# Masking with a byte written into a bf16: TensorE's constant pass left out, key weights scaled by a power of two

## The reference

```python
U = min(L, int(FACTOR * math.log(L)))                # 5 * ln 512 -> 31
Q, K, V = proj(Wq, bq), proj(Wk, bk), proj(Wv, bv)   # 16 x 16 heads x 512 x 16
scores = jnp.einsum('bhqd,bhkd->bhqk', Q, K) / math.sqrt(D)
top_vals, _ = jax.lax.top_k(scores, U)
thresh = top_vals[..., -1:]
scores = jnp.where(scores < thresh, -jnp.inf, scores)
attn = jax.nn.softmax(scores, axis=-1)
x = _layernorm(x + context @ Wo.T + bo)
gate, up = x @ wg.T, x @ wu.T                        # weights are int32 / 127
x = _layernorm(x + (silu(gate) * up) @ wd.T)
```

## Time and profile before

| | |
|---|---|
| median of 3 runs | 3387.09 us (3374.43 to 3392.51) |
| the profiled execution's own time | 3384.81 us |
| its span | 3383.0 us |
| granted TensorE clock, mean | 0.913 |
| busy: PE, DVE, ACT, POOL | 83%, 76%, 71%, 71% |
| tiles per run | 1024, so 3.30 us of span for each |

### The profile page before, as it was taken

One profiled execution on the slowest core, in us unless ns is written; L12 is line 12 of the kernel. 1 busy time (PEld: TensorE's weight loads), 2 busy tenths in 40 slices (PEclk: granted clock), 3 DMA queues, 4 the chain that ended last, 5 costly groups with the idle time before them and its releaser, 6 DMA issues.

```text
span 3383.0 us, 82396 instructions
## 1 busy us (share of the span) xinstructions
PE 2808.2 (83%) x21094; PEld 1534.9 (45%) x21439; DVE 2587.7 (76%) x12511; ACT 2414.3 (71%) x5894; POOL 2405.8 (71%) x1677
## 2 busy tenths in 40 slices
PE   5889899697989888776998999987789976886986
PEld 2344545344444444433544454544445443443454
DVE  4888788787878787777887888887778877777861
ACT  4788787686868787665786788886668865675862
POOL 2787788586777786656786787876668865675881
PEclk7799999899999898987998999998889988898986
DMA  3101011110101111011110111111011110111000
GB/s 82 43 23 43 22 41 31 33 26 19 44 24 35 25 35 35 18 32 23 27 42 21 36 24 46 27 37 32 17 33 27 46 25 15 33 26 27 20 14 7
DMA packets 91071, 102.84 MB, mean 30 GB/s; under 512 B 34417, under 2 KB 52850, under 8 KB 90482
## 3 DMA queue, kind: packets, MB, share of 16 engines
q1 hardware_dynamic: 88448, 93.73, 11.6%
q10 hardware_dynamic: 2034, 2.76, 0.2%
HBM read 20.86 MB, written 8.39 MB: 9 GB/s over the span
## 4 chain that ended last, share of the span: by engine, by line
PE 44%; DVE 19%; issue 15%; ACT 11%; POOL 4%; DVEq 4%; SPq 1%; ACTq 0%; DMA 0%; POOLq 0%
DVE cand L866 6%; PE Y_ps L606 5%; PE bench L676 5%; PE ST_ps L620 5%; PE ST_ps L617 5%; PE ctxT_ps L634 5%; PE bench L670 4%; ACT junk L459 4%; PE Y_ps L604 3%; POOL mask L1088 3%; ACT above L468 3%; DVEq L948 3%; PE bench L547 2%; ACT PT L476 2%; DVE S L859 2%
## 5 line engine op out<-in xcount | busy, mean ns | idle before, releaser
L1088 POOL TENSOR_SCALAR mask<-S,thr,mb 128x512 bf16<-128x512 f32 x1024 | 2117.6, 2084 | 43.0 <-POOL mb L1082 24.8
L866 DVE MAX8 cand<-Y_ps 128x8 f32<-128x128 f32 x4096 | 1069.2, 281 | 9.9 <-issue 9.8
L459 ACT ACTIVATE junk<-S,nt 128x512 bf16<-128x512 f32 x1024 | 733.7, 716 | 476.4 <-DVE S L859 472.9
L859 DVE TENSOR_SCALAR_CACHE_REDUCE S<-S_ps,na 128x512 f32<-128x512 f32 x1024 | 755.6, 738 | 298.8 <-PE S_ps L593 246.4
L468 ACT ACTIVATE above<-S,s,steep 128x512 bf16<-128x512 f32 x1024 | 822.5, 803 | 0.0
L476 ACT ACTIVATE PT<-ST_ps 128x512 f32<-128x512 f32 x1024 | 596.6, 583 | 199.0 <-PE ST_ps L620 196.6
L1080 POOL TENSOR_SCALAR rbig<-rmax 128x8 f32<-128x8 f32 x128 | 31.3, 244 | 755.2 <-DVEq L953 755.1
L617 PE MATMUL ST_ps<-QS,KS 64*128 64x512 f32 x1024 | 463.4, 453 | 94.3 <-ACT PT L476 89.7
L593 PE MATMUL S_ps<-KS,QS 64*128 64x512 f32 x1024 | 532.3, 520 | 4.2 <-DVE S L859 2.2
L606 PE MATMUL Y_ps<-KS,QS 64*128 64x512 f32 x1024 | 532.1, 520 | 1.0 <-issue 0.7
L604 PE MATMUL Y_ps<-above,nbig 128*128 128x512 bf16 x1020 | 406.6, 399 | 146.8 <-DVE cand L866 107.6
(11 more groups left out here) (121 smaller groups left out, 3837.7 us busy)
## 6 DMA issues: line engine op xcount, KB each, us to landing
QS<-Qhi SPq DMA_DIRECT2D x512, 32.0 KB, 2.0
KS<-Khi SPq DMA_DIRECT2D x512, 32.0 KB, 2.0
KS<-Klo SPq DMA_DIRECT2D x512, 32.0 KB, 2.0
QS<-Qlo SPq DMA_DIRECT2D x512, 32.0 KB, 2.0
xTs<-in_xT SPq DMA_DIRECT2D x17, 512.0 KB, 3.8
xs<-in_x SPq DMA_DIRECT2D x16, 512.0 KB, 3.9
out<-xs SPq DMA_DIRECT2D x16, 512.0 KB, 2.9
hT<-in_wgT ACTq DMA_DIRECT2D x1, 768.0 KB
```

Source lines behind the costliest of these rows:

```text
L459: nc.scalar.activation(junk[:, :], S[:, score_place(j)[0], :], ACT.Sign, bias=nt0[:, hb, col:col + 1], scale=-1.0, accum_out=s0[:, j % 8:j ...
L859: nc.vector.tensor_scalar(S[:, at, :], S_ps[n % 2][:, :], na[:, hb, col:col + 1], None, ALU.add, op1=ALU.max, accum_out=rmax[:, n % RING:n ...
L866: mx = nc.vector.max(cand[:, j % CANDS, i, :], Y_ps[j % 2][:, i * BW:(i + 1) * BW])
L1088: nc.gpsimd.tensor_scalar(mask[:, h % MASKS, t, :], S[:, score_place(j)[0], :], thr[:, r:r + 1], mb[:, r:r + 1], ALU.is_lt, op1=ALU.add).t ...
```

## The change

The tile of ones and its pass are gone. `above` is cleared to zero once at the start, and `count_second` writes Sign's output as an unsigned byte into the upper byte of every bf16 element of it. A +1 is to become the byte 1, so that the bf16 has the bits 0x0100, which is 2^-125; a -1 is to become the byte 0, and the element 0. A new diagonal matrix `nbyte` = -2^127 times the identity turns such elements into -4 and 0 in one matmul. So that 4 is far above every score, keys are scaled by `SHIFT` = 2^-38: DVE multiplies the key weights and bias by it once at the start. `BIG` becomes 4, which is 2^40 in the scaled units, the exponential's scale is divided by `SHIFT`, and `TINY`, the floor of the variance, is lowered.

```diff
-BIG = 2.0 ** 40
+SHIFT = 2.0 ** -38
+BIG = 4.0
+BYTE_BIG = 2.0 ** 127
-TINY = 1.0e-30
+TINY = 1.0e-36
-        ones_b = sb("ones_b", [P, L], BF16)
+        nbyte = sb("nbyte", [P, P], BF16)
 # count_second, on ACT
-                nc.scalar.activation(above[:, j % 4, :], S[:, score_place(j)[0], :], ACT.Sign, bias=s0[:, j % 8:j % 8 + 1],
+                nc.scalar.activation(above[:, j % 4, :].bitcast(U8).rearrange("p (l y) -> p l y", y=2)[:, :, 1], S[:, score_place(j)[0], :], ACT.Sign, bias=s0[:, j % 8:j % 8 + 1],
                                      scale=steep[:, hb, col:col + 1], accum_out=s1[:, j % RING:j % RING + 1]).then_inc(cnt1_done, 1)
 # exponentials, on ACT
-                nc.scalar.activation(PT[:, j % 4, :], ST_ps[:, :], ACT.Exp, scale=SCALE).then_inc(exp_done, 1)
+                nc.scalar.activation(PT[:, j % 4, :], ST_ps[:, :], ACT.Exp, scale=SCALE / SHIFT).then_inc(exp_done, 1)
 # below, on PE
-                nc.tensor.matmul(Y[:, :], nbig[:, :], ones_b[:, :], start=True, stop=False)
-                nc.tensor.matmul(Y[:, :], nbig[:, :], above[:, j % 4, :], start=False, stop=False)
+                nc.tensor.matmul(Y[:, :], nbyte[:, :], above[:, j % 4, :], start=True, stop=False)
 # the start, on DVE
-            nc.vector.memset(ones_b[:, :], 1.0)
+            nc.vector.memset(above[:, :, :], 0.0)
             nc.vector.memset(onesc[:, :], 1.0)
             nc.vector.memset(ones[:, :], 1.0)
             dve.wait_ge(w_loaded, 16 * N_W)
             nc.vector.tensor_copy(ident_r[:, :], ident[:, :])
             nc.vector.tensor_copy(heads_r[:, :], heads[:, :])
-            nc.vector.tensor_scalar(nbig[:, :], ident[:, :], -BIG, None, ALU.mult).then_inc(consts_done, 1)
+            nc.vector.tensor_scalar(nbig[:, :], ident[:, :], -BIG, None, ALU.mult)
+            nc.vector.tensor_scalar(nbyte[:, :], ident[:, :], -BYTE_BIG, None, ALU.mult)
+            nc.vector.tensor_scalar(bqk[1][:, :], bqk[1][:, :], SHIFT, None, ALU.mult)
+            nc.vector.tensor_scalar(wqk[1][:, :, :], wqk[1][:, :, :], SHIFT, None, ALU.mult).then_inc(consts_done, 1)
+            dve.wait_ge(consts_done, 1)
```

More of the change, by code:

```diff
@@ L88 @@
 BF16 = mybir.dt.bfloat16
+U8 = mybir.dt.uint8
 ALU = mybir.AluOpType
```

## The result

The changed kernel takes 3417.60 us (median of 8 runs, 3406.22 to 3426.35), the kernel before 3385.31 us in the same comparison: a ratio of 1.0095, 95% interval 1.0076 to 1.0113. I had forecast 3347 us, 1.1% faster, in a range of 3295 to 3415. The time lies outside the range and on the other side of the kernel before.

What follows compares the result with a forecast made beforehand. PE was taken to be late in heavy slots, with DVE, ACT and POOL setting the pace in light ones. 3384.8 - 74 + 33 + 1 = 3345 us, 3347 as a median; range 3295 to 3415.

Steps and rivals of the forecast that it cites:

- The passes on the chain: PE's removed 0.22 us pass per tile, where DVE or ACT waits for PE in heavy slots: 74 us gained.
- 88 (the chain): Upper end of the pass's gain: about 400 of 1024 tiles pass through `below` on the chain, at 0.22 us each.
- What is late next in heavy slots is DVE, and it has room: After PE in heavy slots: DVE's waits for scores average 1.1 us, five times the pass.
- The clock: PE in light slots, doing less work, falls to half clock 65 more times: +33 us, mean clock about 0.88.
- What a fall costs: One fall in a light stretch costs 1.20 us with the pass, 0.3 without; 0.5 us taken.
- rival B: Light slots after a fall and the heavy ones they lead into: clock outweighs the pass, 3444 us; chance 0.12.
- The estimate of 0.44 us returned for each tile: PE at half clock in light slots: the removed pass saves twice 0.22 us, for about two tiles per fall.
- E: PE's light slots stay at 2.4 GHz where they did before: 3314 us, or 3300 with the whole chain; chance 0.12.
- A: The pass was hidden behind other engines: half of 49 us gained, 3396 us, or 3372 with few falls; chance 0.19.
- C: ACT's byte writes cost 0.44 us more for each of 1024 tiles, partly hidden: 3571 us; chance 0.04.
- D: Wrong stored bytes or Sign sums make DVE's whole-tile search run for all tiles: over 2.8 ms extra; chance 0.02.
- The small terms: Start of the kernel: `nbyte`, key bias and key weights scaled by DVE, 0.22 + 0.1 + 0.7 = 1 us.

Runs made afterwards that it cites:

- ACT relieved: Changed kernel with exponential on 256 of 512 columns: pass kept in every slot 3327.1 us, kept only in the 34 light slots 3295.1 us.
- two fillers: Two extra 512-column matmuls, results overwritten, in each of 34 light slots: changed kernel 3362.8 us, kernel before 3407.6 us.
- near and far fillers: Changed kernel, two extra overwritten matmuls per slot: in seven light slots ahead of slots 4, 30, 38, 3376.1 us; in the other 27 light slots, 3410.7 us.
- seven slots with fillers: Changed kernel with two extra overwritten 512-column matmuls in slots 1, 2, 3, 28, 29, 36 and 37 alone: 3376.1 us, ratio 0.9985 to before.

## Why the prediction was wrong

**The passes on the chain: the wrong size.** I took 74 us, from 49 us (DVE's waits) to 88 (the chain). Measured at an almost unchanged clock, leaving them out in the 30 slots with a large product or right behind one gave 17 us, and DVE's wait for the scores fell there from 241.6 to 214.2 us and ACT's for `ST_ps` from 194.8 to 176.3. The failing step is "What is late next in heavy slots is DVE, and it has room". DVE does have room; ACT does not. PE waits for ACT's exponential before it can turn the next scores, because `ST_ps` has one buffer. That wait stood at 89.7 us in 183 places in the kernel before, a row that I did not weigh; only 27 us of it lay in slots with a large product, and without the pass there it became 59. The 88 us was a bound on where the pass stood on the chain, not on what it would give back. With ACT relieved it gave 32. The 74 was for all 64 slots. What the passes give in the 34 light ones can't be told apart from what the clock takes there; with two fillers in these in both kernels, leaving all passes out gave 45 us, but there the fillers themselves make PE later.

**The clock: the right term, too small.** I said that PE stands at the edge in light slots and would fall more often. It did, but not in the shape that I gave it. I counted 65 new falls of 3.4 us, 221 us at half clock, and took +33 us for them. In the traces the stretches at half clock went from 51 to 89, so 38 more, and they last 12 and 11 us on the mean; 3.4 us, which I took from one fall, is about the shortest. Together they grew by 394 us (983 - 589). The measured price: the kernel with the pass only in light slots takes 3370.9, the one without any 3417.6, so taking it out of light slots costs 47 us in net. That is 0.13 us for each of about 370 us more at half clock (0.909 to 0.856), near the 33 / 221 = 0.15 that I had used. So the rate for each us was about right, by luck, since the price of a fall (0.5 us) was too low and its length too: 28 more stretches for 47 us are 1.7 us each. The amount was short.

**What a fall costs: right on the sum, wrong on the reason.** I expected a fall in a light stretch to cost 0.3 us instead of 1.20 without the pass. These two windows of the changed kernel cover the same slots as the first two of the earlier trace rows.

```profile
440.61:457.35 16.74, 14.96 (x102) 7.01 (x101) 15.69 (x85) 13.58 (x33) 16.42 (x13) 0.69 0.24 53
639.50:655.05 15.55, 13.74 (x105) 6.68 (x105) 15.13 (x85) 13.47 (x34) 15.23 (x13) 0.84 0.22 49
```

The first has a clock of 0.69 and the same 16.74 us as the earlier trace rows with the pass. The second was at half clock for a third of its length (0.84), and lasts 15.55 us, as at full clock. Slot by slot, slots 19 to 21 of the first last 2.92, 1.74 and 2.13 us at half clock, and 2.91, 1.75 and 2.13 us at full clock in the kernel before (second stretch of the earlier trace rows). Slots 22 and 23 last 2.72 and 2.78 us, where they take 2.01 and 2.31 in the second. So half clock cost nothing in slots where PE has time to spare, the same 1.2 us as before in the two where it has none, and most in the long slots 4, 30 and 38. The estimate of 0.44 us returned for each tile appears nowhere here. I named the heavy slots in one clause ("a fall can also reach into a heavy slot") and in rival B, and gave them no price of their own. They are where the cost stands: 40 us in slots 4, 30 and 38.

**The rivals.** B, at a chance of 0.12, is what happened in kind and sign, but milder than its 3444 us: the time lies between my forecast and B. E, that the clock holds, is refuted (0.913 to 0.856). In the trace the fall inside slot 30 above comes with no pause of PE longer than 1.00 us in the 10 us before it, so no long idle stretch is needed. The Trainium skill's page "TensorE: Matmul & The Clock Gate" (section "Part 1: The HAM clock gate") has the clock fall once PE has been idle; the trace disagrees, with this fall. The kernels with none, half and all of the pass show that the amount of work in such stretches counts. One more reading was off, in E: the clock was up not in 9 tenths of the run but in 83% of it, since a mean of 0.913 is 589 us at half clock in 3383. A is half true: with the clock held the pass gave 17 us in the 30 slots, close to A's 25, where I had 74. C (806 ns) did not happen. D neither: DVE's whole-tile search ran for 24 tiles, as before.

```profile
L933 DVE MAX8 gtop<-S x24: 695/695/695, 121.8 to 3151.2; 128x8 f32<-128x512 f32 x24
```

**The small terms.** The three new operations at the start took 0.22, 0.16 and 0.42 us in the trace, overlapping; 1 us was an upper figure. They don't matter.

```profile
13.61 0.22 DVE L1062 TENSOR_SCALAR nbyte<-ident 128x128 bf16<-128x128 f32 x1
13.74 0.16 DVE L1063 TENSOR_SCALAR bk<-bk 128x2 f32<-128x2 f32 x1
13.81 0.42 DVE L1064 TENSOR_SCALAR wk<-wk 128x512 f32<-128x512 f32 x1
```

**The sum with measured terms.** Before 3385; bytes and scale +3 (the kernel with the pass kept; by its interval 1 to 10); passes of the 30 slots out -17; those of the 34 light slots out, with the clock that they cost, +47: 3418 us. The terms are differences of medians of a row of kernels, each an edit of the last, so that they close is no proof of its own; each has an uncertainty of some 5 us or more.

**What stays open.** Why a faster stretch of long slots gives back part of its gain in light ones; why the same matmul holds the clock better inside `below` than at the slot's end; how far the 35 us between near and far fillers holds for other sets of slots; and what the pass would give with the clock held everywhere and ACT relieved, which was not tried.

## What to carry to other kernels

Before taking work off TensorE, look at the granted clock of stretches in which it waits for others, and at whether equal stretches of the trace have it at both levels; if so, the work that you remove may also be holding the clock. Price the loss not by the mean clock but by the long stretches of PE work that stand right behind light ones, and keep or add PE work just ahead of these: seven slots with fillers brought back 42 us here. And when a step on the chain is shortened, list every wait of the engine that is freed, not only the waits for it: the next one in line (here ACT's exponential) can cap the gain.

## What was not expected of the hardware

- Adding work that computes nothing made a kernel 2.0% faster (3417.6 to 3350.3 us), at PE busy 87% instead of 83%.
- The granted clock fell although PE had not paused for more than 1.00 us in the 10 us before (the fall in slot 30, at 470.4 us of the changed kernel's trace).
- The mean clock says little of the time without its place: 0.938, 0.931 and 0.930 went with 3407.6, 3387.7 and 3350.3 us, and 0.897 with 3410.7 us but 0.878 with 3376.1.
- ACT writes single bytes two bytes apart at the speed of a dense bf16 output: 806 ns against 803 for 128x512 elements, with an accumulated sum beside it. The sum it accumulates seems to be that of the values ahead of the conversion: had the -1s been summed as 0, the count would be off and DVE's whole-tile search would run more often, and it stayed at 24 tiles.
